# Row sums of ctx: two TensorE transposes and a copy, or a way through DRAM (samples five to eight)

## The reference, cut to what matters

```python
# B = 8 samples, C = 256 channels, D = 1024
xn  = layernorm(x)                                   # over D
t   = einsum('oc,bcd->bod', Wt, ctx); p = einsum('oc,bcd->bod', Wp, xn); g = einsum('oc,bcd->bod', Wg, ctx)
att = sum over each of 8 groups of p * g             # one number per sample and group
y   = groupwise Wz of (att * t); yn = group-normalised y
x   = x + tanh(g_xattn) * (yn * gn_w + gn_b + ctx)
# then a feed-forward part on layernorm(x): router scores, top 16 of 64 experts,
# softmax gate, z = xn A^T (512 wide), gated z times B^T, scaled
x   = x + tanh(g_ffn) * ffn(layernorm(x))
```

## Time and profile before

| | |
|---|---|
| median of 3 runs | 324.51 us (324.15, 324.51, 326.56) |
| the profiled execution, its own time | 325.73 us |
| its span | 323.9 us |
| granted TensorE clock in it, mean | 0.995 |
| PE busy | 319.0 us, 98% of the span |
| DVE busy | 245.9 us, 76% |
| ACT busy | 174.9 us, 54% |
| POOL busy | 168.5 us, 52% |
| DMA | 62.69 MB, mean 194 GB/s |

### The profile page before, as it was taken

The page is one execution under the profiler, slowest core; times in us unless marked ns, Lnnn a source line. Parts: engine busy times, 40 slices in busy tenths (PEclk is TensorE's granted clock), DMA queues, the critical chain, the costliest instruction groups (busy, mean ns, idle before and its releaser), DMA issues.

```text
span 323.9 us, 5543 instructions
## 1 busy us (share of the span) xinstructions
PE 319.0 (98%) x1960; PEld 290.4 (90%) x1960; DVE 245.9 (76%) x636; ACT 174.9 (54%) x298; POOL 168.5 (52%) x158
## 2 busy tenths in 40 slices
PE   8999999999999999999999999999999999999996
PEld 6688998899988999898999899898999889989985
DVE  1856897596588946888887799788987798789362
ACT  3687845677256485286545658177454654354110
POOL 0464699189463969339581677429591580010000
PEclk9998999999999999999999999999999999999999
DMA  7999900990650585249951899228961631272102
GB/s 248 412 388 397 363 4 7 328 306 10 191 200 13 184 300 190 63 134 272 405 200 34 253 358 361 67 89 275 365 252 61 224 134 74 58 244 82 65 32 99
DMA packets 28091, 62.69 MB, mean 194 GB/s; under 512 B 2448, under 2 KB 12560, under 8 KB 28064
## 3 DMA queue, kind: packets, MB, share of 16 engines
q1 hardware_dynamic: 27712, 62.14, 54.6%
q10 hardware_dynamic: 352, 0.20, 0.2%
HBM read 46.34 MB, written 15.99 MB: 192 GB/s over the span
## 4 chain that ended last, share of the span: by engine, by line
PE 94%; DMA 3%; SPq 1%; issue 0%; ACT 0%; DVE 0%
PE z_ps L1266 20%; PE w_ps L1296 18%; PE w_ps L1185 12%; PE w_ps L1266 12%; PE z_ps L1125 9%; PE w_ps L1303 9%; PE z_ps L1104 4%; DMA cT_first<-in_cT 3%; PE t_ps L1213 2%; PE w_ps L1125 2%; PE t_ps L1243 2%; PE t_ps L1280 1%; PE z_ps L1198 1%; PE z_ps L1213 1%; PE t_ps L1342 1%; PE w_ps L1314 0%
## 5 line engine op out<-in xcount | busy, mean ns | idle before, releaser
L1296 PE MATMUL w_ps<-B_hi,zT_hi 128*128 128x512 f32 x124 | 49.3, 397 | 0.0
L1296 PE MATMUL w_ps<-B_lo,zT_hi 128*128 128x512 f32 x124 | 48.4, 391 | 0.0
L384 POOL TENSOR_TENSOR xT_lo<-xT_in,xT_hi 128x512 fp32r<-128x512 f32 x24 | 30.6, 1298 | 20.5 <-ACT xT_hi L500 17.7
L418 POOL TENSOR_TENSOR c_sb<-c_sb,x_sb 128x512 f32<-128x512 f32 x28 | 36.2, 1329 | 6.9 <-ACT c_sb L603 6.9
L403 POOL TENSOR_TENSOR c_lo<-c_sb,c_hi 128x512 fp32r<-128x512 f32 x24 | 30.3, 1292 | 14.1 <-DVE uw L863 14.1
L557 ACT ACTIVATE uw<-w_ps,neg_u 128x512 f32<-128x512 f32 x32 | 20.2, 686 | 28.8 <-DVE neg_u L808 28.8
L574 ACT ACTIVATE hT_hi<-t_ps 128x512 fp32r<-128x512 f32 x32 | 18.5, 599 | 30.7 <-DVE t_ps L884 22.5
L1266 PE MATMUL z_ps<-A_hi,hT_hi 128*128 128x288 f32 x160 | 34.7, 298 | 0.2 <-ACT hT_hi L574 0.2
L1266 PE MATMUL z_ps<-A_lo,hT_hi 128*128 128x288 f32 x160 | 34.1, 294 | 0.0
L1303 PE MATMUL w_ps<-B_hi,zT_lo 128*128 128x512 f32 x124 | 33.3, 390 | 0.0
L384 POOL TENSOR_TENSOR cT_lo<-cT_in,cT_hi 128x512 fp32r<-128x512 f32 x24 | 30.6, 1300 | 2.4 <-DVE uw L863 2.4
(11 more groups left out here) (191 smaller groups left out, 846.8 us busy)
## 6 DMA issues: line engine op xcount, KB each, us to landing
c_sb<-in_ctx SPq DMA_DIRECT2D x16, 512.0 KB, 6.8
x_sb<-in_x SPq DMA_DIRECT2D x16, 512.0 KB, 7.3
xT_in<-in_xT SPq DMA_DIRECT2D x14, 512.0 KB, 6.8
cT_in<-in_cT SPq DMA_DIRECT2D x14, 512.0 KB, 8.1
out_block<-uw SPq DMA_DIRECT2D x14, 512.0 KB, 6.2
w_through<-uw SPq DMA_DIRECT2D x10, 512.0 KB, 3.2
c_sb<-w_through SPq DMA_DIRECT2D x10, 512.0 KB, 4.0
z_through<-zg_sb SPq DMA_DIRECT2D x9, 256.0 KB, 2.3
```

The lines of the kernel that those rows point to most:

```text
L384: last = pool.tensor_tensor(lo[:, chunks, :], came[:, chunks, :], hi[:, chunks, :].bitcast(f32), ALU.subtract)
L418: last = pool.tensor_tensor(c_sb[n % 2][:, t, cols], c_sb[n % 2][:, t, cols], x_sb[:, t, cols], ALU.add)
L1296: pe.matmul(w_ps[k][:, :], zT_hi[:, t, row], w[:, j, cols], start=(j == 0 and w is B_hi), stop=False)
```

## The change

For samples n = 4 to 7 PE's two transposes and ACT's copy of them go. In their place ACT issues two DMAs. `sums_to_dram(n)`, right after the two `c_high(t, n)`, waits for them to be finished and writes `c_sum` to a new DRAM tensor of 256 numbers: 128 pieces of 8 bytes, in the order channel p of tile 0, channel p of tile 1. `sums_to_all(n)`, between the two halves of `w_square`, waits for that write and reads the 1 KB back to each of the 128 partitions of `cb_sb`. As the numbers lie interleaved now, `gram_fix` reads them in steps of 8 bytes from the fifth sample on. Two waits on `cb_s` (in `group_means`, and at the last `out_product` of samples from the third on) fall away or wait for less, since `w_ps[3]` isn't used for it any more; `c_high` gets a wait for the DRAM write of the sample before.

```diff
+        sums_through = nc.dram_tensor("sums_through", (1, C), f32).ap()
...
+        sums_out, sums_in = sem("sums_out"), sem("sums_in")
...
   (c_high)
+                if n > 4:
+                    act.wait_ge(sums_out, 16 * (n - 4))
...
+            def sums_to_dram(n):
+                act.wait_ge(c_hi_s, per_tile(n, T - 1))
+                act.dma_start(sums_through.rearrange("o (p t) -> p (o t)", p=P), c_sum[:, :]).then_inc(sums_out, 16)
+
+            def sums_to_all(n):
+                act.wait_ge(sums_out, 16 * (n - 3))
+                act.wait_ge(M_fixed, per_tile(n - 1, T - 1))
+                act.dma_start(cb_sb[:, :], sums_through.to_broadcast([P, C])).then_inc(sums_in, 16)
...
                 if m + 1 < NB:
                     for t in range(T):
                         c_high(t, m + 1)
+                    sums_to_dram(m + 1)
                 zT_high(0, b)
                 if b < NB - 2:
-                    cb_copy(m + 1)
-                    w_square(m)
+                    w_square(m, (0,))
+                    sums_to_all(m + 1)
+                    w_square(m, (1,))
...
   (gram_fix)
-                dve.wait_ge(cb_s, n + 1)
+                dve.wait_ge(cb_s if n < 4 else sums_in, n + 1 if n < 4 else 16 * (n - 3))
...
+                    if n >= 4:
+                        bank = gram_bank(n, t)[:, 0:C].rearrange("p (i c) -> p i c", i=T)
+                        dve.scalar_tensor_tensor(bank, cb_sb[:, :].rearrange("p (c i) -> p i c", i=T),
+                                                 neg_x[:, t:t + 1], bank, ALU.mult, ALU.add).then_inc(M_fixed, 1)
+                        continue
...
   (group_means)
-                pe.wait_ge(cb_s, n + 1)
+                pe.wait_ge(cb_s, min(n, 3) + 1)
...
   (out_product)
-                if k == USES - 1 and 1 <= n < NB - 2:
+                if k == USES - 1 and n == 1:
                     pe.wait_ge(cb_s, n + 3)
...
   (PE's loop)
-                    gram(m + 1, {(0, 3): lambda: group_means(m), (0, 6): lambda: group_att_var(m),
-                                 (1, KH): lambda: ctx_sums(m + 1)})
+                    gram(m + 1, {(0, 3): lambda: group_means(m), (0, 6): lambda: group_att_var(m)})
```

## The result

The changed kernel takes 333.19 us (median of 4 runs, 332.22 to 335.08) against 325.28 us for the kernel before in the same comparison (4 runs). The ratio estimated from the runs is 1.0257, 95% interval 1.0224 to 1.0289 (the two medians alone give 1.0243): some 8 us slower. I had forecast 323.8 us and a range up to 326.5.

The account below looks back on a forecast made before the run. PE's own instructions were taken as the bound; removing four transpose pairs gave 0.68 us, the added DMAs and strided reads nothing: 324.51 - 0.68 = 323.8 us, range 323.1 to 326.5.

Parts of the forecast that it names:

- The bound: Whole kernel: PE's instruction list plus its waits set the time; PE is busy 98% of the span, 94% of the chain.
- the side chain: ACT and DVE work from w_tiles through w_square(1), offsets, zT_high(1), zT_low(1), gram_fix, hT_turn to hT_high, which PE needs next.
- the slack: Before z_product, PE starts 0.13 us (by load) or 0.17 us (by matmul) later than ACT's and DVE's work would allow.
- What is removed, 0.22 us a pair: PE's transposes in the Gram product: each pair costs 0.22 us, of which 0.17 arrives, 0.68 us over four iterations.
- ACT's issues: Issuing each DMA on ACT takes 0.49 us and costs nothing; 0 to 0.2 if the first takes twice that.
- gram_fix with steps of 8 bytes: Two DVE instructions of 0.48 us: strided reading adds 0, or 0.44 for both if stride explained the slower transpose.
- The bound of 0.22 per instruction: In gram_fix: the most that strided reading might add to each 256-number instruction, 0.44 for two.
- Its landing. I take 2.3.: The small write to DRAM lands 2.3 us after issue; it begins to cost from 2.96 us.
- The rival with the slow write: 8-byte pieces land after 4.6 us, ACT waits, w_square(1) starts 1.8 us late: 331.0 us; chance 0.12 including late broadcast.
- Other queues: a few tenths of sharing I put at nothing.: The new 1 KB and 128 KB join SP's transfers; sharing of a few tenths costs nothing, as w's reads have cover.
- "Its landing", of the broadcast: The 128 KB broadcast lands after 3.2 us, 1.2 us before gram_fix, and costs nothing.
- The 4.4 us of room: The broadcast costs nothing if it lands within 4.4 us of issue, in time for gram_fix.

Follow-up runs that it names:

- e1: The changed kernel without its two DMAs, gram_fix using the fourth sample's row sums for samples five to eight: 0.9963 of the kernel before.
- e10: The changed kernel with each partition writing a whole 32 bytes and all 4 KB read back to each partition: 1.0096 of the kernel before.
- e15: The kernel before plus both DMAs and ACT's wait for the first, the broadcast going to a spare tile, gram_fix not waiting: 1.0187 of the kernel before.
- e2: The kernel before plus only the write of c_sum to DRAM, 128 adjacent pieces of 8 bytes, used by nobody: 1.0181 of the kernel before.
- e4: The kernel before plus only a broadcast of 1 KB from DRAM to a spare tile, waiting for no write: 1.0022 of the kernel before.
- e3: The kernel before plus only the write, each partition writing 512 bytes instead of 8, 64 KB in all: 0.9998 of the kernel before.
- e8: The changed kernel with both DMAs going through one partition of SBUF instead of DRAM: 1.0411 of the kernel before.
- e12: The changed kernel with whole pieces of 16 bytes, 2 KB written and 256 KB read to all partitions: 1.0100 of the kernel before.
- e14: The kernel before plus only a write of 32 adjacent pieces of 8 bytes, 256 bytes in all: 1.0357 of the kernel before.
- e11: The changed kernel with ACT's own summing pass and the round trip ahead of u_copy, and 32-byte pieces: 1.0024 of the kernel before.
- e6: The kernel before plus only a write of 128 pieces of 64 bytes side by side, 8 KB: 1.0008 of the kernel before.
- e5: The kernel before plus only the write of 128 pieces of 8 bytes, each 512 bytes from the next in DRAM: 0.9967 of the kernel before.
- e7: The kernel before plus only the write of 128 pieces of 8 bytes, to one partition of SBUF: 0.9987 of the kernel before.
- e9: The changed kernel with the round trip moved ahead, ACT summing in its own pass before u_copy, 8-byte pieces: 0.9963 of the kernel before.

## Why the prediction was wrong

**The bound, the side chain, the slack.** Right. 1.98 us of lateness on it became 1.79 us of time, a slack of 0.19 where I had 0.13 to 0.17. The 0.06 us for a semaphore in it was my estimate; the rows show 0.03 from DVE's end to ACT's start (181.07 to 181.10), and the chain of the kernel before has 0.04 from the end of ACT's `hT_high` at 32.98 + 0.61 to PE's start at 33.63. With the 0.04 the slack by the matmul is 0.19.

**What is removed, 0.22 us a pair.** Right: 0.19 of it arrives in e1, where I had 0.17. The single transpose's duration, 0.27 for each of two, would have promised nearly three times as much.

**ACT's issues.** Right: 0.33 to 0.35 us each, under the 0.49 I had taken, and `zT_high(0)` starts 0.17 us later against its release, with no cost.

**gram_fix with steps of 8 bytes.** Right, nothing: L806 takes 0.485 us in the mean, L787 took 0.479. The bound of 0.22 per instruction happens to be the price of a step of 32 bytes (e10); that is luck.

**"Its landing. I take 2.3."** This term failed: 3.5 to 4.0 us. I took the nearest row by place and had none of 8-byte neighbours. The rival with the slow write named this and priced it at 4.6 us and 331.0; I gave it 0.12. Its number is near the result, in part by luck. ACT does stand in the wait, and `gram_fix` is late, as the rival's last sentence has it. But the price was reckoned from ACT's late `w_square(1)`, which in e15 shows no cost beside the late z; and the late z, the larger part, isn't in that rival.

**"Other queues: a few tenths of sharing I put at nothing."** This is the step that failed. By itself the held-up z costs 5.9 us (e2) of the 8. The parts overlap and don't simply add: in three of the four iterations the round trip ends a little later still than what waits for z. I asked how many bytes the new DMAs add to the engines, and 1 KB is nothing. I didn't ask what the transfer issued 0.24 us behind the small write would do if the engines couldn't get on with it. That read of z had a room of some 0.4 us on DVE (issued at 177.97, 2.6 us to land, used at 180.98).

**"Its landing", of the broadcast.** The 4.4 us of room were right; alone it lands in 3.8 (e4), in the changed kernel in 5.0 to 6.0 behind the late transfers. With `gram_fix` waiting for it that is the other 2 us or so (1.0257 against e15's 1.0187).

In the iteration b = 4 the changed kernel's chain also goes through a write of z that landed after 7.2 us, and its interval is 40.42. DVE's waits for such a write, of 0.8 to 1.1 us, stand also in the traces of e2, e3, e4, e8, e10, e12, e14 and e15, and not in that of the kernel before. In e3 w is on time (3.2 us), the wait is there once, and no interval of `z_product` is over 37.21 us. So the late w can't be the whole reason, and such a wait alone needn't cost much. The cause stays open.

## What to carry to other kernels

Before adding a small DMA, look at what is issued right behind it on any queue and when it is due: the cost may fall on a transfer that the edit doesn't touch. Adjacent pieces of 8 and of 16 bytes, written to DRAM from 128 partitions, landed here after 3.6 and 2.3 us and made the read of z behind them late (5.5 to 5.9 and 4.3 to 4.7 us instead of 2.6); padded to 32 bytes, or of 8 bytes and 512 bytes apart, they landed after 1.4 and 1.5 and left z on time. So pad or space such pieces, and then check the step with which the reader must walk over them (a `gram_fix` pair took 1.32 us instead of 0.87 with a step of 32 bytes). A round trip through DRAM, 9.0 us in the changed kernel, belongs where the engines have several microseconds before anything else is due; here the same two DMAs, some 8 us earlier in the iteration, turn a loss of 8 us into a gain of just under 1 by the trace, at the price of a pass of ACT of its own.

## What the runs showed of the hardware

- Adjacent pieces in DRAM, 128 in one DMA: landing after 3.6 us with 8 bytes (e2), 2.3 with 16 (e12), 1.4 with 32 (e10; 2.2 in e11, beside a write of z), 1.4 with 64 (e6), 1.6 with 512 (e3). Eight bytes at 512 bytes' distance: 1.5 (e5). Adjacent 8-byte pieces to one partition of SBUF: 1.9 (e7).
- Behind the slow write (128 adjacent pieces of 8 bytes; the changed kernel and e2) DMAs of another queue landed about 3 us late: z after 5.5 to 5.9 us instead of 2.6, w's writes after 5.9 and 5.6 in the median instead of 3.2. One issued 0.28 us ahead of it was late too (e9: 4.0 instead of 2.3).
- 32 adjacent pieces of 8 bytes (e14) stalled the read of z longer than 128 did (e2): landing after 6.9 to 7.1 us against 5.7 to 5.9, DVE's longest wait for it 4.0 against 2.9 us; why is open.
- A broadcast of 1 KB to 128 partitions landed after 3.8 us from DRAM (e4) and after 7.5 us from one partition of SBUF (e8).
- DVE read f32 from SBUF in steps of 8 bytes about as fast as adjacent ones (0.485 against 0.479 us for 256, PSUM as the other operand and the target); with steps of 16 and of 32 bytes a pair of such instructions took 1.25 and 1.32 us instead of 0.87 (e12, e10).
